# The first two pairs of an attention kernel: orders of four engines written anew, and one weight split moved

## The reference

```
x = x + Wo( softmax( (LN(x) Wq + bq) (ctx Wk + bk)^T / sqrt(128) ) (ctx Wv + bv) ) + bo   # 32 heads of 128, 8 key/value heads
x = x + sum over the top 2 of 8 experts: gate * Bm_e (A_e LN(x)) * 0.5
```

## Time and profile before

| | us |
|---|---|
| median of 3 runs (lowest, highest) | 1047.58 (1045.67, 1048.67) |
| the profiled execution | 1048.27 |
| its span, first to last instruction | 1046.4 |
| TensorE busy in the span | 1025.0 |
| VectorE busy in the span | 801.0 |

### The profile page before, as it was taken

The page is one execution under the profiler, slowest core; times in us unless marked ns, Lnnn a source line. Parts: engine busy times, 40 slices in busy tenths (PEclk is TensorE's granted clock), DMA queues, the critical chain, the costliest instruction groups (busy, mean ns, idle before and its releaser), DMA issues.

```text
span 1046.4 us, 17352 instructions
## 1 busy us (share of the span) xinstructions
PE 1025.0 (98%) x5409; PEld 850.0 (81%) x5409; DVE 801.0 (77%) x1410; ACT 561.2 (54%) x1324; POOL 686.5 (66%) x573
## 2 busy tenths in 40 slices
PE   8999999998999999999999999999999999999997
PEld 7878887877888888888888888888888888888885
DVE  3563455469997988798879878887988797888985
ACT  3032113257766666566567566666666665565423
POOL 1186237778876886678668757876787678575304
PEclk9999999999999999999999999999999999999999
DMA  9646963996383746456463828273746456350004
GB/s 318 206 127 234 322 212 94 377 348 235 114 293 104 261 144 226 150 210 229 142 253 108 299 87 315 99 263 120 251 149 215 175 193 245 117 162 11 1 1 161
DMA packets 85658, 197.99 MB, mean 189 GB/s; under 512 B 10560, under 2 KB 43368, under 8 KB 70384
## 3 DMA queue, kind: packets, MB, share of 16 engines
q1 hardware_dynamic: 83072, 181.73, 50.3%
q10 hardware_dynamic: 2544, 15.73, 3.8%
HBM read 161.78 MB, written 35.65 MB: 189 GB/s over the span
## 4 chain that ended last, share of the span: by engine, by line
PE 80%; DVE 7%; DMA 6%; POOL 3%; ACT 1%; issue 1%; SPq 1%; ACTq 0%; DVEq 0%
PE banks L1746 24%; PE banks L1747 23%; PE banks L1748 23%; PE banks L1898 5%; PE banks L1874 3%; PE banks L1873 3%; DMA k_raw<-keys_dram 2%; PE banks L1773 1%; DVE stats L1278 1%; DMA values_dram<-parts 1%; DMA keys_dram<-parts 1%; POOL xo L629 1%; DVE xo L1203 1%; POOL w_l L629 1%; DMA raw<-in_L_xattn_Wkv_dram 1%
## 5 line engine op out<-in xcount | busy, mean ns | idle before, releaser
L1746 PE MATMUL banks<-wo_h,xo 128*128 128x512 f32 x512 | 204.5, 399 | 0.8 <-DVE y L1685 0.6
L629 POOL TENSOR_TENSOR qT_l<-parts,qT_h 128x512 fp32r<-128x512 f32 x128 | 165.2, 1296 | 57.9 <-ACT qT_h L860 57.9
L1747 PE MATMUL banks<-wo_l,xo 128*128 128x512 f32 x512 | 200.5, 392 | 0.0
L1748 PE MATMUL banks<-wo_h,xo 128*128 128x512 f32 x512 | 199.9, 390 | 0.0
L1746 PE MATMUL banks<-xo,w_h 128*128 128x512 f32 x448 | 176.7, 394 | 1.0 <-DVE parts L1328 1.0
L1747 PE MATMUL banks<-xo,w_h 128*128 128x512 f32 x448 | 174.9, 390 | 0.0
L1748 PE MATMUL banks<-xo,w_l 128*128 128x512 f32 x448 | 174.3, 389 | 0.0
L629 POOL TENSOR_TENSOR xo<-sT,xo 128x512 fp32r<-128x512 f32 (+1 forms) x72 | 102.6, 1425 | 69.2 <-ACT xo L860 69.2
L1203 DVE TENSOR_TENSOR xo<-banks,xo 128x512 fp32r<-128x512 f32 (+1 forms) x156 | 100.7, 665 | 33.5 <-ACT xo L860 33.0
L1746 PEld LDWEIGHTS banks<-wo_h,xo 128*128 128x128 f32 x512 | 96.5, 188 | 24.2 <-DVE y L1685 0.6
L1748 PEld LDWEIGHTS banks<-wo_h,xo 128*128 128x128 f32 x512 | 96.5, 188 | 21.0
(11 more groups left out here) (163 smaller groups left out, 2277.3 us busy)
## 6 DMA issues: line engine op xcount, KB each, us to landing
xo<-x_dram SPq DMA_DIRECT2D x105, 1024.0 KB, 6.2
x_dram<-xo ACTq DMA_DIRECT2D x14, 1024.0 KB, 11.8
values_dram<-parts SPq DMA_DIRECT2D x64, 128.0 KB, 2.9
keys_dram<-parts SPq DMA_DIRECT2D x32, 256.0 KB, 4.8
k_raw<-keys_dram SPq DMA_DIRECT2D x32, 256.0 KB, 4.9
raw<-in_L_xattn_Wo_dram SPq DMA_DIRECT2D x8, 1024.0 KB, 8.0
v_raw<-values_dram SPq DMA_DIRECT2D x64, 128.0 KB, 3.6
raw<-in_L_xattn_Wkv_dram SPq DMA_DIRECT2D x7, 1024.0 KB, 6.5
```

The costliest lines, as they stand in the source:

```text
L629: return nc.gpsimd.tensor_tensor(dst, src, high_part.bitcast(F32), ALU.subtract)
L1746: mm(dst, stat[0], mov[0], start=start, stop=False)
L1747: mm(dst, stat[0], mov[1], start=False, stop=False)
L1748: return mm(dst, stat[1], mov[0], start=False, stop=stop)
```

## The change

Arithmetic, tiles and memory stay. Moved are: on ScalarE, `split_wv(1)` from ahead of the first x tile to behind it; on VectorE, step 3's four `combine_w` from behind K(3,0,2) to behind K(3,1,0) and K(3,1,1); on SP, `load_keys(0, 1, 1)` from behind the block of op 3 to ahead of it; on TensorE, one product and the output tiles against `outputs` and `scores`; and in `opening` the rest of the two pairs on ScalarE, VectorE and GpSimd. The diff, with the long lists cut:

```diff
@@ sync, opening @@
                     if op == 0:
                         sp.wait_ge(resid_ready, TILES)
                         load_values(0, 0, 0)
-                load_keys(0, 1, 1)
+                    elif op == 1:
+                        load_keys(0, 1, 1)
@@ gpsimd, opening @@
                 keys_low(1)
+                normalise(0, 0)
                 shift(0, 1)
-                normalise(0, 0)
                 probs_low(0, 0)
+                normalise(0, 1)
                 split_wo(STEPS, [2])
                 query_low(1, "c11", 0)
-                normalise(0, 1)
+                probs_low(0, 1)
                 query_low(1, "c11", 1)
-                probs_low(0, 1)
                 split_wo(STEPS, [3])
                 shift(1, 0)
-                keys_low(2)
                 query_low(1, "c21", 0)
                 query_low(1, "c21", 1)
+                normalise(1, 0)
+                keys_low(2)
+                probs_low(1, 0)
                 shift(1, 1)
-                normalise(1, 0)
                 values_low(1)
-                probs_low(1, 0)
                 query_low(1, "c22", 0)
...
@@ scalar, opening @@
                 exponents(0, 0)
                 swap_max(0, 1)
                 swap_sum(0, 0)
+                act.wait_ge(block_stored[6], 16 * DUOS)
+                probs_high(0, 0)
                 exponents(0, 1)
+                copy_half(1, 0)
+                swap_sum(0, 1)
                 split_wo(STEPS, [2])
                 query_high(1, "c11", 0)
-                act.wait_ge(block_stored[6], 16 * DUOS)
-                probs_high(0, 0)
-                copy_half(1, 0)
-                swap_sum(0, 1)
-                query_high(1, "c11", 1)
...
@@ scalar, start @@
                     step, i = name[1], name[2] * KVH + name[3]
-                    if i == 0:
-                        act.wait_ge(ring_filled, n)
+                    if i == (5 if step == 0 else 0):
+                        act.wait_ge(ring_filled, pos["K", step, 0, 0])
                         if step + 1 < STEPS:
                             split_wv(step + 1)
@@ vector, opening @@
                 s_sum(0, 0)
+                y_sum(1, 1, 1)
                 s_peak(0, 1)
-                y_sum(1, 1, 1)
                 s_inverse(0, 0)
...
                 query_sum(1, 1, "c21", 0)
+                s_inverse(0, 1)
                 s_add(1, 0)
-                s_inverse(0, 1)
-                s_max(1, 0)
                 p_turn(0, 1)
                 output_low(0, 0, 0)
+                output_low(0, 0, 1)
                 query_sum(1, 1, "c21", 1)
+                s_max(1, 0)
                 w_sum(1, 1, 0)
+                query_sum(1, 1, "c22", 0)
                 s_peak(1, 0)
...
@@ vector, start @@
-                if name == ("K", STEPS - 1, 0, 2):
-                    for what in (1, 2, 3, 4):
-                        combine_w(0, what, True)
+                if name == ("K", STEPS - 1, 1, 0):
+                    combine_w(0, 1, True)
+                    combine_w(0, 2, True)
+                if name == ("K", STEPS - 1, 1, 1):
+                    combine_w(0, 3, True)
+                    combine_w(0, 4, True)
@@ tensor, opening @@
                 product(0, 1, 4, 0)
+                product(0, 1, 4, 1)
                 outputs(0, 0)
-                product(0, 1, 4, 1)
...
                 out(1, 1, 0)
+                out(1, 1, 1)
                 scores(1, 0, 0)
-                out(1, 1, 1)
+                out(1, 1, 2)
                 outputs(1, 0)
-                out(1, 1, 2)
+                out(1, 1, 3)
                 scores(1, 0, 1)
-                out(1, 1, 3)
+                out(1, 1, 4)
                 outputs(1, 1)
-                out(1, 1, 4)
                 out(1, 1, 5)
                 scores(1, 1, 0)
                 out(1, 1, 6)
```

More of the change, by code:

```diff
@@ L744, in opening @@
                 keys_low(3)
-                shift(2, 1)
                 split_q(1, [0], False)
                 normalise(2, 0)
+                shift(2, 1)
+                probs_low(2, 0)
+                values_low(2)
+                normalise(2, 1)
                 split_q(1, [2], False)
-                probs_low(2, 0)
-                normalise(2, 1)
-                split_q(1, [1], False)
-                values_low(2)
                 probs_low(2, 1)
-                split_q(1, [3], False)
-                split_q(1, [5], False)
+                split_q(1, [1, 3, 5], False)
                 shift(3, 0)
-                split_q(1, [4], False)
-                split_q(1, [6], False)
+                split_q(1, [4, 6], False)
             def duo(g, p):
@@ L1471, in opening @@
                 add_out(0, 0, 1, out_slot(1, 1))
+                s_add(2, 0)
+                s_sum(1, 1)
                 s_inverse(1, 1)
[L1473 removed]
+                output_low(1, 0, 0)
+                output_low(1, 0, 1)
                 p_turn(1, 1)
                 s_max(2, 0)
[L1476 to L1477 removed]
+                add_out(0, 0, 2, out_slot(1, 2))
+                add_out(0, 0, 3, out_slot(1, 3))
+                s_peak(2, 0)
                 s_add(2, 1)
[L1479 removed]
                 s_max(2, 1)
+                s_sum(2, 0)
+                output_low(1, 1, 0)
+                output_low(1, 1, 1)
+                s_inverse(2, 0)
+                add_out(1, 1, 0, out_slot(1, 4))
+                s_peak(2, 1)
+                p_turn(2, 0)
+                add_out(1, 1, 1, out_slot(1, 5))
                 combine_w(1, 1, False)
+                s_sum(2, 1)
+                s_add(3, 0)
                 combine_w(1, 2, False)
[L1483 to L1498 removed]
+                s_inverse(2, 1)
+                add_out(1, 1, 2, out_slot(1, 6))
+                add_out(1, 1, 3, out_slot(1, 7))
+                p_turn(2, 1)
+                combine_w(1, 3, False)
+                s_max(3, 0)
+                s_add(3, 1)
                 combine_w(1, 4, False)
[L1500 to L1502 removed]
             def duo(g, p):
```

84 lines of the change are left out of this document (28 added, 56 removed).

## The result

The changed kernel takes 1049.73 us (median of 16 runs, 1047.94 to 1056.49), the kernel before 1047.59 (16 runs, 1045.01 to 1050.03). The ratio is 1.0024, 95% interval 1.0012 to 1.0035: about 2.5 us slower by the ratio and 2.1 by the medians, where 3.0 us faster was forecast.

The account below looks back on a forecast made before the run. TensorE, busy 98%, was taken as the bound, so only waits and half clock, near 7.0 us, could go; 1.1 (start) + 1.9 (pairs) = 3.0 off 1047.58 gave 1044.6, range 1040.4 to 1048.8 (8 in 10).

Parts of the forecast that it names:

- Weights of step 1: Split moved behind the first x tile: TensorE's wait at 54.70 goes, with some restart, a gain of 1.1 us.
- Combinations and keys: Keys emptied before VectorE's combinations, unit 1's keys loaded earlier: lead of 0.4 us, unit 0's chain 1.4 us earlier.
- cap of 0.4 us by op 3's block: Op 3's block would land behind the keys, at 230.17, limiting TensorE's lead up to there to 0.4 us.
- outputs(0, 0) and outputs(1, 0): First without a wait, 1.8 us of idle time gone with the second product's; new wait of 1.3 for 1.97 at the second.
- Output tiles 4 and 6, last scores: Tiles now nearer to the outputs they need: new waits of 1.0 us, 1.1 us and, at the last scores, 0.7 us.
- Hand-over: Written-out pairs to loop: 1.2 us of slack at tile 0; TensorE keeps 1.9 us if VectorE comes 0.7 us earlier.
- Half clock: The 3.41 us at 1.2 GHz behind the wait at 256.86 would go, a gain of 1.7 us.
- VectorE against GpSimd: Shared ports: two more meetings of 0.75 us, at s_peak(1,1) and s_peak(2,0), would make the gain 1.5 us smaller.
- The slower one, VectorE late at the loop: VectorE starting the loop at 290.2 or later makes the kernel slower by over 0.3%, priced at 1051; chance 0.11.
- signs of being wrong: VectorE's copy to g_bias beyond 287, the 54.70 wait back at the next transfer, or new waits under 0.3 us each.
- faster by over 0.3%: Time below 1044.4, chance 0.48: all of the all-waits-go rival (0.20) and somewhat under two thirds of the forecast's case.
- the forecast's case: The main case: 3.0 us faster, 1044.6, own range 1043.0 to 1046.2, chance 0.46.

Follow-up runs that it names:

- e1: Kernel before with only the split of step 1's weights moved, behind tile 5 of its keys; 1046.76 us, ratio 0.9992.
- e4: Kernel before with only unit 1's keys loaded behind op 1's block and VectorE's first combinations behind the second unit's keys; ratio 0.9985.
- e11: e8 with one output tile on TensorE moved from behind outputs(1, 0) to ahead of it; ratio 0.9992.
- e3: Changed kernel with swap_max(3, 0) on ScalarE ahead of the split of the last weight block; ratio 1.0007.
- e16: Changed kernel with copy_half(2, 0) and exponents(1, 1) earlier on ScalarE, s_sum(1, 1) and s_max(2, 0) earlier on VectorE; ratio 1.0013.
- e8: Kernel before with the moved split of step 1's weights, the earlier keys and later combinations, all other lists old; 1045.48 us, ratio 0.9983.
- e2: Changed kernel with the split of step 1's weights put back ahead of the first x tile; ratio 1.0024.
- e14: Changed kernel with VectorE's later query-weight combinations made over 8 of 256 columns, the rest left out; ratio 1.0001.
- e17: e16 with swap_max(3, 0) ahead of the last split as in e3; 1047.99 us, ratio 1.002.
- e6: Changed kernel with TensorE's old order of output tiles 1 to 4 against unit 1's scores and outputs; ratio 1.007.
- e10: Changed kernel with the old lists up to the second s_inverse of unit 1, new ones behind, TensorE's new order kept; ratio 1.0005.
- e15: Changed kernel with the old order of all four engines up to outputs(0, 0), new ones behind; ratio 1.0042.
- e9: Changed kernel with new lists up to the second s_inverse of unit 1, old ones behind, TensorE's new order kept; ratio 1.0025.

## Why the forecast was wrong

- **Weights of step 1: right at its place, uncertain in what is kept.** The wait at 54.70 went, and TensorE gained 1.24 us there, against 1.1 forecast. (The 2.1 us at instruction 600 are more than that place gives: 0.33 stood ahead of it, the rest came behind it.) The forecast expected the later transfers to move along: they did in twelve profiles of 17 with this step. By the medians 0.8 us is kept (`e1`), and the interval reaches no gain at all.
- **Combinations and keys: right, and too small.** ScalarE's `kT` comes at 224.54 us against 230.19, of which 2.07 are the lead that TensorE brings from the start. The cap of 0.4 us by op 3's block did not hold: that block was issued at 210.40, where the keys had been at 213.30, and TensorE starts its product at 227.74 against 230.59 before, without a wait, 2.85 us ahead. Alone, this part gives 1.6 us (`e4`).
- **outputs(0, 0) and outputs(1, 0): right.** The first has no wait; the second has 0.25 us, where 1.3 were forecast. With the early part alone the second stays at 2.0 us, and with one tile moved (`e11`) it is gone, so the tile did remove it.
- **Output tiles 4 and 6, last scores: right.** Forecast 1.0, 1.1 and 0.7 us, measured 0.84, 0.96 and 0.38 idle, by the releasers named.
- **Hand-over: the step that failed.** "TensorE keeps 1.9 us only if VectorE comes 0.7 us earlier, which is a tenth of its idle time; I take that." The condition was met, and TensorE did not keep the time: VectorE came at 282.83, as the text had it ("at 283"), and TensorE's lead fell from 5.11 us at the loop's first product to 1.96 at the fifth, the start's gain included. The limit was read at the wrong place. Slack was counted at tile 0 of the loop, 299.43, but TensorE comes to the fifth product 12.4 us before that (287.06), and there it waits for ScalarE's copy, which stands behind the last split and so behind VectorE's last combination. Moving one step there gives 1.7 us (`e3`). VectorE, too, came at 282.83 only because it began earlier: from its first `s_add` on it was 0.8 us slower than before, not faster, and 1.8 in the second profile. (Its idle time on that way was 5.87 us before, not 7.3: the window that was read began 1.41 us ahead of its first `s_add`.) I summed the waits of TensorE and took VectorE's list to run without gaps of its own. The order of the change showed `s_inverse(1, 1)` next to `s_sum(1, 1)`, and `copy_half(2, 0)` behind queries that VectorE makes. Those two gaps are 2.1 us; without them others of 1.1 come, and the kernel is 1.1 us better by its ratio (`e16`), with overlapping intervals.
- **Half clock: it moved.** Its 1.7 us were booked as gained for good; it came back behind the wait at 285.10 in both profiles of the changed kernel, and took 1.6 us of the lead there.
- **VectorE against GpSimd: the meetings came, no loss shown from them.** `s_peak(1, 1)` takes 1.16 us at 249.57 and `s_peak(2, 0)` 0.90 at 261.78, where 0.17 was read for one alone. VectorE's copy of 128x4 at the hand-over took 1.23 us, where it took 0.30 before; it ended at 284.06, and GpSimd's, in this row of the changed kernel, at 284.04:

```profile
282.31 1.73 POOL L630 TENSOR_TENSOR w_l<-raw,w_h 128x512 fp32r<-128x512 f32 x1
```

By the Trainium skill's rule (SBUF — State Buffer, section SBUF: two separate sides) a VectorE instruction in a two-port mode or with two SBUF inputs and one of GpSimd hold the shared pair of ports one after the other, each for the whole instruction. The trace agrees with the rule; that the copy runs in such a mode no row shows. But the twelve small steps of this kind on VectorE's way to the loop take 6.34 us together, against 5.43 before and 6.74 in `e8`, and its busy time (58.34 us) is no more than in `e8` (58.89), so the meetings do not explain the loss against `e8`.

- **The rivals.** The slower one, VectorE late at the loop, had the right place at a chance of 0.11. Its condition (VectorE at 290.2 or later) was wrong, since it asked for VectorE's arrival and not for ScalarE's release of the bank. The signs of being wrong missed it too: in the first profile none of the three came (a copy beyond 287, a wait at the next transfer, new waits all under 0.3 us), and the kernel is slower by its median. Apart from this, the chance of 0.48 for "faster by over 0.3%" does not follow from its terms: it takes nearly two thirds of the forecast's case, whose own value, 1044.6, lies above the limit of 1044.4, so less than half of it belongs there, some 0.4 in all.

Shown: the pairs with the new lists lose (`e2`), the early part gains (`e4`), and without the new lists the change is faster than before (`e8`); the place of `swap_max(3, 0)` carries 1.7 us of the loss, and VectorE's load ahead of the hand-over counts (`e14`). Likely, with overlapping intervals: that the start gains 0.8 us and that VectorE's two gaps carry 1.1. Open: whether these two losses add (`e17` can't tell), and the rest between `e17` and `e8`. Also open is why in some profiles a block of x lands late (0.3 to 2.1 us of waiting near 219 to 231 us) and in others not.

## What to carry to other kernels

Where a second engine is nearly as busy as the bound one in a stretch, sum that engine's own list too: each step that is put next to the step it depends on, through a third engine, is a gap on it, and the bound engine may pay for it at the end of the stretch. A lead of the bound engine is worth only what its partners' arrival at the next shared point allows, and that point is the first buffer it needs back, whichever engine empties it. When a change is a bundle, time its parts: here three small edits give 1.8 us, and the new orders around them take some 4 away.

## What the runs showed of the hardware

The half clock does not follow each wait. After the wait of about 1.9 us at the loop's fifth product it came in five profiles (the changed kernel twice, `e6`, `e10`, `e15`) and stayed away in two with the same wait (`e2`, `e16`). At outputs(1, 0) it came after 1.97 and 1.98 us in three (before, `e1`, `e4`) and stayed away after 1.99 in `e8`. In the tail of `e16` it came at 1024.01, behind a wait of 0.65 us, which the kernel before (at 1022.74) and the changed one (at 1022.39) have without it. Beside waits of 3.9 and 4.0 us it stayed for 6.83 us (`e9`, `e6`). So one profile with or without it proves little of an order: it was worth 1.6 us of TensorE's lead behind 285.10.

An addition of 16 columns on VectorE took 1.00 us beside a running GpSimd instruction (`e14`), and ended with it at 282.5; one took 0.15 at 271.41 in the same profile, between two of GpSimd's.
